# An adaptive-layernorm transformer block: columns of x and x1 by way of DRAM and 32x32 transpositions, instead of TensorE

## What is computed

```python
mod = (silu(c) @ wmod).reshape(4, 6, 1, 512)
sa, ca, ga, sb, cb, gb = ...            # six vectors for each batch
ga = sign(ga) * max(|ga|, 0.25)         # gb the same
h = layernorm(x) * (1 + ca) + sa
x = x + ga * attention(h)               # x1
h = layernorm(x) * (1 + cb) + sb
out = x + gb * (sum_r h @ factors[r] / sqrt(8) + bias)
```

## Time and profile before

| | us |
|---|---|
| runs | 524.8, 522.56, 520.8 |
| median | 522.56 |
| span of the profiled execution, first to last instruction | 523.7 |
| TensorE busy in it | 500.1 |
| VectorE busy | 346.4 |
| ScalarE busy | 276.7 |
| GpSimd busy | 192.9 |

### The profile page before, as it was taken

One profiled execution on the slowest core, in us unless ns is written; L12 is line 12 of the kernel. 1 busy time (PEld: TensorE's weight loads), 2 busy tenths in 40 slices (PEclk: granted clock), 3 DMA queues, 4 the chain that ended last, 5 costly groups with the idle time before them and its releaser, 6 DMA issues.

```text
span 523.7 us, 9716 instructions
## 1 busy us (share of the span) xinstructions
PE 500.1 (95%) x2506; PEld 407.4 (78%) x2506; DVE 346.4 (66%) x638; ACT 276.7 (53%) x579; POOL 192.9 (37%) x286
## 2 busy tenths in 40 slices
PE   8988899689999999999999999999999999999985
PEld 3756668468888888888888888888888888888864
DVE  2888877557666666766676666667666665667565
ACT  2875754536466655555564666554555545434531
POOL 0465654252233333333332333333333213223414
PEclk9998999979999999999999999999999999999999
DMA  8877999700202020110202020201001010110102
GB/s 310 319 274 166 213 180 208 141 1 2 80 0 80 0 80 0 40 40 0 80 0 80 0 80 0 78 2 41 0 1 40 1 41 1 40 41 0 40 0 82
DMA packets 17217, 36.41 MB, mean 70 GB/s; under 512 B 1320, under 2 KB 2088, under 8 KB 16944
## 3 DMA queue, kind: packets, MB, share of 16 engines
q1 hardware_dynamic: 13248, 28.60, 15.2%
q0 software_dynamic: 3808, 7.34, 8.1%
q10 hardware_dynamic: 144, 0.26, 0.1%
HBM read 27.80 MB, written 8.40 MB: 69 GB/s over the span
## 4 chain that ended last, share of the span: by engine, by line
PE 78%; DVE 6%; issue 6%; ACT 3%; POOL 3%; DMA 2%; ACTq 0%; SPq 0%; DVEq 0%; POOLq 0%
PE ps_o L315 11%; PE ps_o L317 11%; PE ps_o L316 10%; PE ps_t L321 9%; PE ps_y L315 5%; PE ps_y L316 5%; PE ps_y L317 5%; PE ps_v L315 4%; PE ps_v L316 4%; PE ps_v L317 4%; PE ps_s L389 3%; PE ps_s L390 3%; DMA f_sum<-in_factors 2%; PE ps_qk L315 1%; POOL f_sum L1045 1%
## 5 line engine op out<-in xcount | busy, mean ns | idle before, releaser
L1003 POOL TENSOR_SCALAR ve<-mv 128x1 f32<-128x1 f32 x64 | 15.8, 247 | 265.4 <-DVE mv L795 178.0
L549 ACT ACTIVATE h_f<-ps_t,mod_t 128x128 f32<-128x128 f32 x252 | 95.0, 458 | 32.9 <-PE ps_t L321 32.2
L315 PE MATMUL ps_o<-v_lo,pt_hi 128*128 (+1 forms) x256 | 105.1, 411 | 1.1 <-DVE pt_lo L717 1.1
L317 PE MATMUL ps_o<-v_hi,pt_hi 128*128 (+1 forms) x256 | 100.5, 393 | 0.0
L316 PE MATMUL ps_o<-v_hi,pt_lo 128*128 (+1 forms) x256 | 99.7, 390 | 0.0
L595 ACT ACTIVATE x2n<-x_ring,nmr,rstd 128x512 f32 (+1 forms) x32 | 26.0, 812 | 84.3 <-POOL nmr L1007 84.3
L317 PEld LDWEIGHTS ps_o<-v_hi,pt_hi 128*128 128x128 f32 x256 | 48.0, 188 | 11.0
L315 PEld LDWEIGHTS ps_o<-v_lo,pt_hi 128*128 128x128 f32 x256 | 48.2, 188 | 9.4 <-issue 1.3
L316 PEld LDWEIGHTS ps_o<-v_hi,pt_lo 128*128 128x128 f32 x256 | 48.3, 189 | 8.6
L717 DVE TENSOR_TENSOR v_lo<-ps_v,v_hi 128x512 f32 (+1 forms) x28 | 19.3, 690 | 52.3 <-ACT v_hi L544 52.2
L770 DVE CAST h_hi<-h_f 128x512 fp32r<-128x512 f32 (+1 forms) x35 | 14.6, 416 | 57.0 <-ACT h_f L549 54.3
(11 more groups left out here) (157 smaller groups left out, 1007.8 us busy)
## 6 DMA issues: line engine op xcount, KB each, us to landing
x_ring<-in_x SPq DMA_DIRECT2D x16, 512.0 KB, 3.4
result<-x_ring SPq DMA_DIRECT2D x15, 512.0 KB, 2.8
f_sum<-in_factors POOLq DMA_DIRECT2D x14, 512.0 KB, 7.0
wmod<-in_wmod SPq DMA_DIRECT2D x12, 512.0 KB, 6.8
gates<-gate_rows SPq DMA_DIRECT2D x2, 1024.0 KB, 6.4
wv_raw<-in_wv SPq DMA_DIRECT2D x4, 256.0 KB, 7.9
wo_raw<-in_wo_t SPq DMA_DIRECT2D x4, 256.0 KB, 8.0
f_sum<-in_factors SPq DMA_DIRECT2D x1, 1024.0 KB, 5.3
```

The source lines that it names most:

```text
L315: nc.tensor.matmul(acc, a_hi, b_lo, start=first, stop=False)
L317: return nc.tensor.matmul(acc, a_hi, b_hi, start=False, stop=last)
L549: last = nc.scalar.activation(to[:, k, :], source[:, P * k:P * (k + 1)], ACT.Identity, scale=mod_t[:, b, v + 1, k:k + 1], bias=mod_t[:, b, ...
L1003: nc.gpsimd.tensor_scalar(ve[:, one], mv[:, u, 1:2], EPS, None, ALU.add).then_inc(ve_done, 1)
```

## The change

Three things change.

1. The columns of x from tile q = 9 on, and of x1 for tiles 0 to 29, no longer come from TensorE. ScalarE normalises into `xn` with its columns reordered in 32-column blocks (one tile `xn` for both, where there were two). SyncE sends `xn` to a DRAM tensor of four blocks of 128 x 128 (512-byte pieces) and fetches it back to `xb` or `x1b` with 2 KB for each partition, so that each 32x32 block lies at its transposed place. One VectorE instruction transposes the 64 blocks of 32x32 in place. `modulate_turned` then reads them from SBUF and writes `h_f` or `h2_f` with a stride of four elements. The last two tiles of x1, and x before tile 9, stay on TensorE.
2. `feed_forward(t - 2)` moves from behind `transpose_probs` to just ahead of `attend`, and `transpose_x` and `transpose_h2` leave the steps.
3. On VectorE `gate_attention`, `add_x` and the statistics of x1 for tile t - 1 move from the end of a step to the head of the next, and `h2_parts(t - 2)` stands behind them, ahead of `probs_rest`. `ffn_out` moves behind `row_max` and the new transposition. GpSimd's order follows. Some small tiles of the prologue share the memory of `probs`.

```diff
+            def blocks_out(blocks, rows, done, count, out_sem):
+                wait_alone(sp, sp_passed, done, count)
+                sp.dma_start(blocks.rearrange("a p x -> p a x"),
+                             rows[:].rearrange("p (a x) -> p a x", a=Q)).then_inc(out_sem, 16)
+            def blocks_in(to, blocks, loaded):
+                sp.dma_start(to[:], blocks.rearrange("a (c b) x -> (a c) (b x)", b=Q)).then_inc(loaded, 16)
...
+            def step(g, u, next_x=True, next_norm=True, older=True, store=True, load=False):   # SyncE
+                t = 2 * g + u
+                if next_x:
+                    fetch_x(t + TB + 1, 1 - u)
+                if u == 0 and store:
+                    store_pair(g - 2)
+                if older:
+                    send_x1(t - 1, 1 - u)
+                    fetch_x1(t - 1, 1 - u)
+                if u == 0 and load:
+                    wait_alone(sp, sp_passed, y_stored, 16 * (g - 1))
+                    load_x(g - 2 + 2 * PB)
+                if next_norm:
+                    send_x(t + TB + 2, u)
...
                 t = 2 * g + u                                                              # TensorE
-                transpose_probs(t, prep)
-                if older == 2:
-                    feed_forward(t - 2)
+                transpose_probs(t)
...
-                if next_x:
-                    pe.wait_ge(pt_lo_done, 2 * t + 2)
-                    transpose_x(t + TB + 1)
-                if scores_early:
-                    pe.wait_ge(mod_t_done, 4)
-                attend(t, g, t - 1 if older else None)
+                if older == 2:
+                    feed_forward(t - 2)
+                attend(t, g)
...
+            def modulate_turned(to, source, b, v):                                         # ScalarE
+                turned = source[:].rearrange("p (b k c) -> p k b c", b=Q, c=BLK)
+                for k in range(C):
+                    last = nc.scalar.activation(to[:, k, :].rearrange("p (c b) -> p b c", b=Q), turned[:, k],
+                                                ACT.Identity, scale=mod_t[:, b, v + 1, k:k + 1],
+                                                bias=mod_t[:, b, v, k:k + 1])
...
                 if prep:
                     values(t + TB)
-                if next_x:
-                    modulate_x(t + TB + 1, batch_of(g + u + PB))
...
+                exponentials(t + 1, 1 - u)
+                if u == 0 and not last_pair:
+                    pair_q(g + 1)
+                if next_x:
+                    modulate_x_turned(t + TB + 1, batch_of(g + u + PB))
+                if next_norm:
+                    normalize_x_blocks(t + TB + 2, u)
                 if older:
                     modulate_x1(t - 1, batch_of(g - 1 + u))
-                if next_norm:
-                    normalize_x(t + TB + 2, u)
...
+            def turn_x1(t):                                                                # VectorE
+                dve.wait_ge(x1b_loaded, 16 * (t + 1))
+                nc.vector.transpose(x1b[:], x1b[:]).then_inc(x1b_turned, 1)
...
                 t = 2 * g + u
-                probs_rest(t, 0)
                 if older:
+                    gate_attention(t - 1, 1 - u, batch_of(g - 1 + u))
+                    add_x(t - 1)
                     x1_stats(t - 1, 1 - u)
-                probs_rest(t, 1)
                 if older == 2:
-                    ffn_out(t - 2)
+                    h2_parts(t - 2)
+                for half in range(2):
+                    probs_rest(t, half)
+                if next_norm:
+                    if u == 0:
+                        wait_alone(dve, dve_passed, x_loaded, 16 * (g + PB + 2))
+                    x_stats(t + TB + 2, u)
...
+                if next_x:
+                    turn_x(t + TB + 1)
+                if older == 2:
+                    ffn_out(t - 2)
                 if next_x:
                     h_parts(t + TB + 1, g + u + PB, 1 - u)
                 if late is not None:
                     late()
                 if older:
-                    h2_parts(t - 1)
-                gate_attention(t, u, batch_of(g))
-                if not (last_pair and u == 0):
-                    add_x(t)
+                    turn_x1(t - 1)
```

212 lines of the change are left out of this document (134 added, 78 removed).

## The result

The changed kernel takes 586.59 us in the median of four runs (584.56 to 588.84), the kernel before 523.68 in four beside them (520.8 to 525.84). The ratio is 1.119, with a 95% interval of 1.1132 to 1.1248. Predicted were 530.1 and a range of 520 to 544. The sign was right, the size was not: between the profiled spans lie 60.6 us where 7.5 were worked out.

The account below looks back on a forecast made before the run. TensorE's own queue was taken to bound both kinds of steps. From the 523.7 us span, -0.9 - 10.9 - 0.4 + 15.7 + 2.5 + 1.5 gave 531.2; the median, 1.1 below, was forecast at 530.1, range 520 to 544.

Parts of the forecast that it names:

- Steps with preparation: First loop, ten pairs of steps: a VectorE/ScalarE loop replaces TensorE as bound, 27.7 a pair against 28.79, -10.9 us.
- cast and lo part 1.04: First loop, VectorE: h's cast and lo part behind ScalarE's modulation, priced at 1.04 us of a 13.7 us step.
- An even step from one gating to the next: First loop: the VectorE/ScalarE instructions added up from one attention gating to the next, start to start, 13.7 us.
- took the same: First loop, odd steps: q's rounding gone, qk's parts added ahead of the row maximum, length assumed equal to an even step's.
- The transposition and the trip: VectorE's 32x32 transposition, 0.69 long and 0.61 in a row; DRAM trip 2.1 to 4.2 out, 2.1 back, hidden.
- Strided stores: `modulate_turned` storing four f32 apart pays each element twice: 0.56 a step, 1.1 a pair, +11, 541; chance 0.07.
- D: Rival: VectorE and ScalarE slower than priced, by strided stores (541), dear transposition (540 to 551) or late trip; chance 0.18.
- Steps without preparation: Second loop, seven steps: the feed-forward waits for h2's parts behind the gating, 88.9 against 73.2, +15.7 us.
- the term 12.7: Second loop: closed round from attend's last matmul over gating, statistics, h2 and feed-forward to the next, 12.7 against 10.46 a step.
- rival E: Second loop: TensorE's clock falls too, as it idles 2.7 us each step; seven times 1.5, +10.5, 541; chance 0.08.
- -0.9, between +2 and -2: Start, steps 0 to 2: only step 2's two lost transposition groups count, -0.9; first trips share queues with the factors' sums.
- Here the order costs what it saves above: Second loop: with no values or qk to hide it, the feed-forward's wait for h2 is exposed, +15.7 over seven steps.

Follow-up runs that it names:

- e14: Kernel before with only ScalarE's rounding of q moved behind the modulation of x1, all transpositions on TensorE: 525.40 us, ratio 0.9993.
- e1: Changed kernel with GpSimd's two instructions of `result` working on one column instead of 512: 566.53 us, ratio 1.0814.
- e8: e2 with GpSimd's add of its result, in steps with preparation, waiting until VectorE has written h's lo part: 559.72 us, ratio 1.0662.
- e2: Changed kernel with VectorE making the lo parts of q and k in odd steps right behind h2's parts: 576.23 us, ratio 1.1023.
- e7: e2 with nine unread matmuls between scores and feed-forward in steps without preparation: 568.45 us, ratio 1.0793.
- e12: Changed kernel with early keys (e2), GpSimd's add behind h's lo part (e8) and nine filling matmuls (e7) together: 551.64 us, ratio 1.0500.
- e5: Kernel before in its own order, with x alone taking the trip over DRAM from tile 9 on: 532.07 us, ratio 1.0114.
- e9: e5 with tiles 9 and 10 still transposed by TensorE, so the first trip is tile 11's: 519.04 us, ratio 0.9894.
- e6: Kernel before with TensorE's feed-forward moved to just ahead of attend, `ffn_out` and GpSimd's result later, all transpositions on TensorE: 537.04 us, ratio 1.0217.
- e3: Changed kernel with VectorE making h2's parts of t - 2 ahead of the gating of t - 1, in every step: 650.26 us, ratio 1.2443.

## Why the prediction was wrong, point by point

**What bounds the kernel before**: right. TensorE was full, and e14 shows that a shorter ScalarE chain gives nothing there.

**Steps with preparation**: wrong, and the failed steps were two. The first is the term "cast and lo part 1.04". It measured 2.03 (271.15 to 273.18), in all 20 steps: about 20 us. Taken away, it gave back 17.7 in the ten pairs in e1 and 17.5 in e8. A duration from the earlier trace rows was taken to a place where GpSimd works at the same time, and I had read GpSimd's order only for what waits for it, not for what it runs beside. e1 and e8 show the cause twice, once by less work and once by another time. The Trainium skill's page "SBUF — State Buffer", section "Who interferes with whom", says that a VectorE instruction with two SBUF inputs, or a copy or cast in its two-port modes, and a GpSimd instruction that reads SBUF block each other whole, the later one waiting. The traces agree: 1.64 for 0.69, 1.10 for 0.43, 1.40 for 0.29, and 1.84 for 1.29 the other way. The prediction had no rival of this kind.

The second is the batch edge. "An even step from one gating to the next" looked at a step in the middle. Every eighth step needs the keys made in the same step, and VectorE has them 10.2 us into the step, behind gating, statistics, h2 and pt_lo, where before had them after 7.2. Steps 7 and 15 cost 8.5 us more than regular ones and step 23 lost 2.8 where -0.4 was expected; e2 gave back 11.2 in the ten pairs and step 23.

The rest of the sum held but for two terms. Without the standing lo part a pair is 29.1 (e1), against 27.7: in even steps VectorE waits 0.7 for v_hi, since ScalarE stands in x1's normalisation ahead of it; in odd ones the parts of qk add 1.3 and the missing rounding of q gives back only 0.86, where I "took the same". The mechanism, a loop of VectorE and ScalarE of some 14 us that takes TensorE's place, was right. Of the 53 us between the sum and the measured spans, about 41 lie in the ten pairs (some 19 the standing lo part, 14 these two terms and small ones, 8.5 the batch edges), 3.2 in step 23, 4.7 in the second loop and 4.4 at the start.

**The transposition and the trip**: right in the loops. 0.63 in a row against 0.61; 2.3 us out and 2.7 back (medians), against 2.1 to 4.2 and 2.1. In the second loop the transposition does wait for its DMA, 19.6 us in seven steps, which the prediction had named as a sign of being wrong. But each gating behind such a wait still waits for attend's last matmul, by 0.44 to 2.34 us, and e7 and e12 have the forecast round of 12.7 with the same trips. So it is hidden, though by little: 0.37 of the 0.44 is what the reciprocal and the registers leave idle anyway. **Strided stores** (part of D): a real cost, 0.12 a tile, too small to count. Reading the blocks from SBUF in place of PSUM made the rest of the way from 1.51 to 1.76: 0.13, against the 0.15 forecast.

**Steps without preparation**: the term 12.7 was right to 0.2 (e7). What was added is rival E, to which I gave 0.08: the clock fell in three of the seven steps, at 1.2 to 1.4 us each (in e2 in five). My reason against it was that the one gap shown before a fall was longer, 3.47 against 2.7. One row doesn't show that a shorter gap is safe, and the rival should have had far more.

**Step 31**: +4.0 predicted, +4.1 measured.

**The start**: the term "-0.9, between +2 and -2" was wrong by 4.4, of which some 3 can be chance. The first trip runs beside loads and sums, and a price of 2.1 from the earlier trace rows, the last and lonely transfer of the kernel, doesn't hold there: 10.8. That a later first trip cures it was shown in the order of before (e5 and e9), not in that of the change.

**The reordering**: "Here the order costs what it saves above" held in the second loop, and e6 divides it: the late feed-forward costs nothing there (10.47 a step) as long as TensorE transposes x1 and h2's parts are made in the old place. What costs 2.2 a step is the wait for h2's parts behind the gating, and e3 shows that with x1's trip they can't simply go ahead of it. In the first loop the late feed-forward costs by itself: e6 is 2.2% slower than before. The trip of x in the old order is worth 1.1% (e9). The trip of x1 in the old order, and the gating's new place alone, weren't tried, so what they are worth stays open.

## What to carry to other kernels

When an edit moves instructions of VectorE or GpSimd, lay the two engines' timelines over each other at the new places, and look at durations as well as waits: an instruction that stands still for another engine's shows as busy. Price the exceptional steps (first, last, at a batch's edge) by themselves, from what they need that a middle step doesn't. Take work off the bound engine without changing its order first; a transfer that replaces it should start only when the loads of the prologue are over (e5 against e9).
